# One step of a recurrent cell on one core: tanh straight from the gates, cell update behind it, 250 steps per pass of the loop

## What is computed

```
i = sigmoid(x_t @ U_i + b_i + h @ V_i)
g = tanh   (x_t @ U_c + b_c + h @ V_c)
o = sigmoid(x_t @ U_o + b_o + h @ V_o)
c = h * c + i * g
h = o * tanh(c)
```

## Time and profile before

| | us |
|---|---|
| runs: median (lowest to highest) | 21,944.94 (21,944.29 to 21,952.03) |
| the profiled execution, first to last instruction | 21,945.0 |
| recurrent steps in it, first tanh of the cell (L2048) to the last | 10,610.8 to 21,884.0 |
| TensorE busy over the span | 14,346.5 (65%) |
| VectorE busy | 11,129.5 (51%) |
| ScalarE busy | 7,575.7 (35%) |

### The profile page before, as it was taken

How to read it: one execution, slowest core, us unless ns; L and a number is a source line. 1 busy time by engine, 2 the same in 40 slices (tenths; PEclk the granted TensorE clock), 3 DMA queues, 4 the chain that set the end, 5 groups by cost and what they waited for, 6 DMA issues and landing times. The chain is left out here.

```text
span 21945.0 us, 718236 instructions
## 1 busy us (share of the span) xinstructions
PE 14346.5 (65%) x259448; PEld 11105.6 (51%) x259449; DVE 11129.5 (51%) x57848; ACT 7575.7 (35%) x56505; POOL 6072.3 (28%) x6737
## 2 busy tenths in 40 slices
PE   5417878714864565656777777777777777777776
PEld 3212246512543444444566666666666666666665
DVE  6416666631125545454555555555555555555555
ACT  0007841100110020100455555555555555555554
POOL 1676666675526747476000000000000000000000
PEclk9558977757986777777555555555555555555555
DMA  0000012301013333333000000000000000000000
GB/s 29 15 5 5 1 48 82 74 14 44 24 41 103 102 76 102 75 103 86 6 4 4 4 4 4 4 4 4 4 4 4 4 4 4 4 4 4 4 4 15
DMA packets 344758, 617.89 MB, mean 28 GB/s; under 512 B 152419, under 2 KB 222154, under 8 KB 340328
## 3 DMA queue, kind: packets, MB, share of 16 engines
q0 software_dynamic: 251520, 473.04, 8.5%
q1 hardware_dynamic: 89704, 98.43, 1.4%
HBM read 506.71 MB, written 64.29 MB: 26 GB/s over the span
## 5 line engine op out<-in xcount | busy, mean ns | idle before, releaser
L2024 PE MATMUL lr_Z<-ls_h,ls_V 128*128 128x1 f16 x225000 | 7186.5, 166 | 3316.4 <-DVE ls_h L2071 2623.7
L2024 PEld LDWEIGHTS lr_Z<-ls_h,ls_V 128*128 128x128 f16 x225000 | 6667.9, 105 | 4152.9 <-DVE ls_h L2071 3442.9
L2065 DVE SCALAR_TENSOR_TENSOR ls_c<-ls_S,ls_hc 128x1 f32<-128x1 f32 x12500 | 2374.0, 220 | 4116.6 <-ACT ls_S L2041 4116.6
L2040 ACT ACTIVATE ls_S<-lr_Z 128x1 f32<-128x1 f32 x12500 | 2070.6, 171 | 5260.5 <-PE lr_Z L2024 5260.5
L1985 POOL COPY ls_HT<-ls_h 128x50 f32 x250 | 56.3, 225 | 11233.4 <-DVE ls_h L2073 11233.4
L620 PE MATMUL prop_sum<-prop_G,prop_S 128*128 128x256 f32 x5040 | 1894.5, 555 | 1676.1 <-DMA prop_G<-hop_table,prop_idx 1276.1
L607 POOL DMA_INDIRECT prop_G<-hop_table,prop_idx x2520 | 2386.5, 947 | 1355.1 <-issue 804.5
L620 PEld LDWEIGHTS prop_sum<-prop_G,prop_S 128*128 128x128 f32 x5040 | 1426.1, 290 | 2144.4 <-issue 991.3
L2071 DVE TENSOR_TENSOR ls_h<-ls_S,ls_th 128x1 f16<-128x1 f32 x12500 | 1879.9, 163 | 817.4 <-ACT ls_th L2048 49.4
L2048 ACT ACTIVATE ls_th<-ls_c 128x1 f32<-128x1 f32 x12500 | 2098.4, 199 | 0.0
L2045 ACT ACTIVATE ls_S<-lr_Z 128x1 f32<-128x1 f32 x12500 | 2068.7, 171 | 0.0
(11 more groups left out here) (407 smaller groups left out, 15623.5 us busy)
## 6 DMA issues: line engine op xcount, KB each, us to landing
prop_G<-hop_table,prop_idx POOLq DMA_INDIRECT x2520
hop_table<-gnn_H SPq DMA_DIRECT2D x3, 6400.0 KB, 20.3
me_W<-in_L_ffn_W SPq DMA_DIRECT2D x16, 1024.0 KB, 10.9
moe_out<-me_Ys SPq DMA_DIRECT2D x108, 128.0 KB, 1.7
gm_AG<-gat_atable,gm_idx POOLq DMA_INDIRECT x840
gs_G<-gat_table,gs_idx POOLq DMA_INDIRECT x840
sd_records<-sc_ring_recsd,sc_ring_placesd POOLq DMA_INDIRECT x784, 2.1
ss_records<-me_ring_recss,me_ring_placess POOLq DMA_INDIRECT x432, 2.1
```

The source lines that it names most:

```text
L2024: mm = nc.tensor.matmul(Z[hf][bank][:, col:col + 1], (V2 if part == "21" else V1)[:, q, ROWS.index(row), :], hx[:, prev, q:q + 1], start=F ...
L2040: nc.scalar.activation(S[:, s % 2, m:m + 1], Z[hf][m][:, col:col + 1], ACT.Sigmoid, scale=back)
L2065: nc.vector.scalar_tensor_tensor(c[:, e, m:m + 1], S[:, e, KD + m:KD + m + 1], S[:, e, m:m + 1], hc[:, m:m + 1], ALU.mult, ALU.add).then_i ...
```

## The change

What it does:
- ScalarE makes tanh(c) itself from the gates, as tanh(g * i + hc): input g, scale i, bias hc, all 128x1 in memory. It waits for hc at the start of a step and for its own gate activations before each tanh.
- Its order becomes g0, i0, g1, i1, tanh 0, o0, tanh 1, o1. VectorE's h1 waits for o0 and o1.
- VectorE still makes c, for hc only. h2 is made per half, as tanh * o - h1 in one operation of the kind of L2065, each with its own semaphore, ahead of h. TensorE waits for each half of h2 apart, and only ahead of the first matmul that needs a new one, so 4 waits stand in a step instead of 36.
- h1 and h2 are kept for two steps instead of 50.
- One pass of the loop has 250 steps in parts of 125, so there are 25 passes instead of 125, and `ahead` is 48 matmuls of 125 columns per part.
- The table of activation functions is loaded once ahead of the loop by an instruction of its own.

```diff
-HALF = 25
+HALF = 125
 BODY = 2 * HALF
...
-        h1 = ph.sb("h1", [P, BODY, KD], F16)
-        h2 = ph.sb("h2", [P, BODY, KD], F16)
+        h1 = ph.sb("h1", [P, 2, KD], F16)
+        h2 = ph.sb("h2", [P, 2, KD], F16)
...
-                            hf, prev = s // HALF, (s - 1) % BODY
+                            hf, prev = s // HALF, (s - 1) % 2
...
-                                hx, made = (h2, h2_made) if part == "12" else (h1, h1_made[q])
-                                if (part == "12", q) not in waited:
-
+                                hx, made = (h2, h2_made[q]) if part == "12" else (h1, h1_made[q])
+                                if made not in waited:
                                     pe.wait_ge(made, i * BODY + s + 1)
                                     waited.append(made)
...
+                    nc.scalar.preload_act_table(ACT.Sigmoid)
                     with act.Fori(0, N // BODY) as i:
                         for s in range(BODY):
-                            hf, col, t = s // HALF, s % HALF * KD, i * BODY + s
+                            hf, col, t, e = s // HALF, s % HALF * KD, i * BODY + s, s % 2
+                            act.wait_ge(hc_made, t + 1)
                             for m in range(KD):
                                 act.wait_ge(z[m], t + 1)
-                                nc.scalar.activation(S[:, s % 2, m:m + 1], Z[hf][m][:, col:col + 1], ACT.Sigmoid, scale=back)
-                                nc.scalar.activation(S[:, s % 2, KD + m:KD + m + 1], Z[hf][m][:, col + 1:col + 2], ACT.Tanh,
-                                                     scale=back).then_inc(gates[m], 1)
+                                nc.scalar.activation(S[:, e, KD + m:KD + m + 1], Z[hf][m][:, col + 1:col + 2], ACT.Tanh, scale=back)
+                                nc.scalar.activation(S[:, e, m:m + 1], Z[hf][m][:, col:col + 1], ACT.Sigmoid, scale=back).then_inc(gates[m], 1)
                             for m in range(KD):
+                                act.wait_ge(gates[m], t + 1)
+                                nc.scalar.activation(th[:, e, m:m + 1], S[:, e, KD + m:KD + m + 1], ACT.Tanh, bias=hc[:, m:m + 1],
+                                                     scale=S[:, e, m:m + 1])
                                 act.wait_ge(z[2 + m], t + 1)
-                                nc.scalar.activation(S[:, s % 2, 2 * KD + m:2 * KD + m + 1], Z[hf][2 + m][:, col:col + 1], ACT.Sigmoid, scale=back)
-                            for m in range(KD):
-                                act.wait_ge(cell[m], t + 1)
-                                nc.scalar.activation(th[:, s % 2, m:m + 1], c[:, s % 2, m:m + 1], ACT.Tanh).then_inc(tanh_made[m], 1)
+                                nc.scalar.activation(S[:, e, 2 * KD + m:2 * KD + m + 1], Z[hf][2 + m][:, col:col + 1], ACT.Sigmoid,
+                                                     scale=back).then_inc(o_made[m], 1)
...
-
-                                nc.vector.scalar_tensor_tensor(c[:, e, m:m + 1], S[:, e, KD + m:KD + m + 1], S[:, e, m:m + 1], hc[:, m:m + 1],
-                                                               ALU.mult, ALU.add).then_inc(cell[m], 1)
+                                cell = nc.vector.scalar_tensor_tensor(c[:, e, m:m + 1], S[:, e, KD + m:KD + m + 1], S[:, e, m:m + 1],
+                                                                      hc[:, m:m + 1], ALU.mult, ALU.add)
+                            cell.then_inc(c_made, 1)
...
                             for m in range(KD):
-                                dve.wait_ge(tanh_made[m], t + 1)
-                                nc.vector.tensor_tensor(h1[:, s, m:m + 1], S[:, e, 2 * KD + m:2 * KD + m + 1], th[:, e, m:m + 1],
+                                dve.wait_ge(o_made[m], t + 1)
+                                nc.vector.tensor_tensor(h1[:, e, m:m + 1], S[:, e, 2 * KD + m:2 * KD + m + 1], th[:, e, m:m + 1],
                                                         ALU.mult).then_inc(h1_made[m], 1)
+                            for m in range(KD):
+                                dve.wait_ge(h1_made[m], t + 2)
+                                nc.vector.scalar_tensor_tensor(h2[:, e, m:m + 1], th[:, e, m:m + 1], S[:, e, 2 * KD + m:2 * KD + m + 1],
+                                                               h1[:, e, m:m + 1], ALU.mult, ALU.subtract).then_inc(h2_made[m], 1)
                             nc.vector.tensor_tensor(h[:, s, :], S[:, e, 2 * KD:M6], th[:, e, :], ALU.mult).then_inc(h_made, 1)
                             dve.wait_ge(h_made, t + 1)
-                            nc.vector.tensor_tensor(h2[:, s, :], h[:, s, :], h1[:, s, :], ALU.subtract).then_inc(h2_made, 1)
+                            dve.wait_ge(c_made, t + 1)
                             nc.vector.tensor_tensor(hc[:], h[:, s, :], c[:, e, :], ALU.mult).then_inc(hc_made, 1)
```

More of the change, by code:

```diff
@@ L1975, in lstm_layer @@
             z = [pr.sem(f"z{g}") for g in range(BANKS)]
-            gates, cell, tanh_made, h1_made = ([pr.sem(f"{n}{j}") for j in range(KD)] for n in ("gates", "cell", "tanh", "h1_"))
-            h_made, h2_made, hc_made, kept = (pr.sem(n) for n in ("h", "h2", "hc", "kept"))
+            gates, o_made, h1_made, h2_made = ([pr.sem(f"{n}{j}") for j in range(KD)] for n in ("gates", "o", "h1_", "h2_"))
+            c_made, h_made, hc_made, kept = (pr.sem(n) for n in ("c", "h", "hc", "kept"))
             with pr.block() as block:
@@ L2053, in _ @@
                     for m in range(KD):
-                        nc.vector.memset(h1[:, BODY - 1, m:m + 1], 0.0).then_inc(h1_made[m], 1)
-                    nc.vector.memset(h2[:, BODY - 1, :], 0.0).then_inc(h2_made, 1)
+                        nc.vector.memset(h1[:, 1, m:m + 1], 0.0).then_inc(h1_made[m], 1)
+                        nc.vector.memset(h2[:, 1, m:m + 1], 0.0).then_inc(h2_made[m], 1)
                     nc.vector.memset(hc[:], 0.0).then_inc(hc_made, 1)
```

## The result

The changed kernel takes 22,775.75 us (22,771.88 to 22,779.15) against 21,944.61 of the kernel before (21,940.15 to 21,952.03): a ratio of 1.0379, 95% interval 1.0364 to 1.0394, slower. The forecast was 22,800 (22,350 to 23,300). The profiled execution has 22,769.8, so 824.8 more than the 21,945.0 of before.

The account below looks back on a forecast made before the run. The bound was a ring of dependent small operations, 1.70 us per step, plus the loop's turns. 21,945 + 1,370 for longer steps - 516 for fewer turns + 5 at the start = 22,800 us, range 22,350 to 23,300.

Parts of the forecast that it names:

- The ring: Recurrent stage: dependent small operations across TensorE, VectorE and ScalarE, 1.70 us once round, 6,250 times, plus the loop's turns.
- Fewer turns, -516: Recurrent loop: turns after the first pass go from 124 to 24, 100 x 5.16 us saved.
- Table load, 0: Loop's turn: the 1.28 us load lies wholly beside TensorE's stall, so taking it out saves 0.
- Tanh 0.38: ScalarE's cell tanh: 0.20 us plus 0.09 for each of two operands in memory; next activation starts 0.29 after it.
- First h1 at 0.77: VectorE's first h1 starts 0.77 us after the step's first gate, where it was 0.78.
- Second half 0.36 behind: VectorE's second h1 starts 0.36 us behind the first, where it was 0.14.
- 18th matmul at 0.90: TensorE's 18th matmul of a step can start 0.90 us after the first h1 starts.
- two waits +0.07: ScalarE ahead of g0: waits for both hc and the gates' matmuls add 0.07 us (bounds 0 and 0.09).
- The sum: Whole step: 0.77 + 1.17 = 1.94 us, taken as 1.92, +0.22 per step, +1,370 over 6,226 steps; total 22,800.
- B: Rival on ScalarE's tanh: both operands cost one read, tanh 0.29, step 1.74, total 21,680 us; chance 0.12.
- C: Rival on ScalarE's tanh: operands cost nothing, tanh stays 0.20, step 1.54, total 20,430 us; chance 0.06.
- D: Rival on VectorE: hc is late and holds the gate, step 2.00 to 2.03, total 23,300 to 23,500 us; chance 0.08.

Follow-up runs that it names:

- loop_alone: Kernel before with 250 steps per pass (parts of 125) and nothing else of the change: 23,122.7 us against 23,641.5, ratio 0.978.
- the run with one operand: Changed kernel with the cell tanh's scale a constant and hc still its bias: 23,289.4 us, where the kernel before takes 23,641.5.
- the run with none: Changed kernel with bias and scale of the cell tanh as constants: 22,200.0 us, where the kernel before takes 23,641.5.
- new_step_short_pass: Changed kernel with 50 steps per pass, as before: 24,969.7 us, +1,328 against the kernel before, ratio 1.056.
- hc_wait_at_tanh: Changed kernel with ScalarE's wait for hc moved from the step's start to the first tanh: 22,400.2 us against 21,963.9 of the kernel before, ratio 1.020.
- low_half_alone: Kernel before with h2 made per half in one operation ahead of h, each half with its own wait: 21,878.9 us against 21,963.9, ratio 0.9963.
- the attempt at a better order: Kernel before with 250 steps per pass, h2 per half and ScalarE's order o0 tanh0 o1 tanh1: 21,299.4 us against 21,963.9, ratio 0.9701.
- table_load_alone: Kernel before with the activation table load taken out of the loop and nothing else: 21,964.8 us against 21,963.9, ratio 1.0001.

## Why the prediction was right, point by point

**What bounds it.** The ring was the right picture: the changes of a step's time in the eight runs above are those of the ring, and no engine became the bound (TensorE is busy 73% of the stage in the changed kernel). TensorE's granted clock is 0.50 in it from 12,000 to 15,000 and from 18,000 to 21,000 us, as before.

**Fewer turns, -516.** Right: -514 in the trace of the changed kernel, -519 by the loop alone. A turn did not get cheaper: it costs between 5.1 and 5.7 in all ten traces, with passes of 50 steps and of 250.

**Table load, 0, and work ahead, 0 in the loop.** Right, the first measured by itself, the second by the steps of 1.700 in loop_alone. The first tanh of the stage comes 3.6 later; 5 were in the sum, for the wider matmuls at the start.

**Tanh 0.38.** Right: 0.386, and the o-gate starts 0.29 after it. This was the step that carried the forecast, and the row that decided it was VectorE's, not ScalarE's. That row gave 0.07 for a second operand; the 0.09 that was taken was the price of ScalarE's first one once more, a guess that the run with one operand confirms. By the Trainium skill, "ScalarE: Activation LUTs", section "What ACT_TABLE_LOAD costs", each pointer operand adds about 93 ns; the runs agree, 91 and 92.

**First h1 at 0.77.** It is at 0.74. The four gate activations start 0.07, 0.05, 0.05 apart, not 0.07 each, but the tanh waits for the semaphore of its gate, to 0.27, so only 0.01 of that arrives; the rest is the o-gate, which lasts 0.15 behind a tanh, not 0.17.

**Second half 0.36 behind, 18th matmul at 0.90, two waits +0.07.** 0.33, 0.89 and +0.07, and the next gate 1.16 behind the first h1 where 1.17 was forecast. The second half of h2 is made 0.14 behind the first, as forecast. The mechanism was the one that shows, with TensorE waiting twice inside a step, for the second h1 and for the second half of h2. Three narrow windows on the matmuls of the step above show it:

```profile
18002.16 0.38 PE L2023 MATMUL lr_Z<-ls_h,ls_V 128*128 128x1 f16 x8 [0.58 <-DVE ls_h L2072]
...
18002.49 0.38 PE L2023 MATMUL lr_Z<-ls_h,ls_V 128*128 128x1 f16 x8
...
18002.78 0.27 PE L2023 MATMUL lr_Z<-ls_h,ls_V 128*128 128x1 f16 x4
```

At the pace of each group of eight the 9th matmul would start at .40 and the 17th at .73; they start at .49 and .78. Against the kernel before, the first h1 gains 0.03, the 18th matmul comes 0.17 later behind it, and the second wait ahead of the first gate costs 0.07: together the 0.20.

**The sum.** The step was put at 1.92 and is 1.90: 0.02 x 6,226 = 125 us too much. Left out were the longer steps, 88 us more than before. The two errors nearly cancel. Luck is in the 1.92 too: the terms as they stand give 1.94, and the 0.02 was taken off for rounding, without a row. With 1.94 the sum is some 22,930, still in the range, but 150 too long; the terms that were too long are those of the first h1 (0.03) and of what follows it (0.01). So the 24 us between 22,800 and 22,776 say less for the sum than its terms do.

**The rivals.** B is excluded by the run with one operand. C is what the run with none shows, 1.533 against its 1.54: had the operands been free, the change would have done what it says. D did not come as the rule: the first gate starts 0.12 after hc has ended in the step shown (18002.82 + 0.16 = .98 to 18003.10). The waits of the changed kernel, 12,000 to 22,500 us, name hc 130 times:

```profile
ACT ls_S L2041 <- PE lr_Z L2023: 4700.1, 5293, 6.6
...
ACT ls_S L2041 <- DVE ls_hc L2081: 115.2, 130, 0.9
```

Over the whole stage these are 150 gates, at six places of a pass. At two of them (50 gates) hc is 0.16 late and the gate 0.08 to 0.09: there D is real, and they are among the longer steps below. At the other four the gate is not late.

**What was missed: the longer steps.** In each pass of 250 the same 18 steps are 0.08 to 0.35 longer, in every pass alike. Two of them, near the 85th and the 97th of a pass:

```profile
11744.66 0.16 DVE L2072 TENSOR_TENSOR ls_h<-ls_S,ls_th 128x1 f16<-128x1 f32 x1 [0.17 <-ACT ls_S L2048]
11745.11 0.35 DVE L2076 SCALAR_TENSOR_TENSOR ls_h<-ls_th,ls_S,ls_h 128x1 f16<-128x1 f32 x2 [0.29 <-issue]
```

```profile
11766.81 0.17 ACT L2042 ACTIVATE ls_S<-lr_Z 128x1 f32<-128x1 f32 x1
11767.09 0.17 ACT L2041 ACTIVATE ls_S<-lr_Z 128x1 f32<-128x1 f32 x1
```

VectorE stands 0.29 ahead of L2076 for nothing that the profile shows, and ScalarE starts its third gate 0.28 behind the second, where it is else 0.05. The runs narrow it. It isn't the length of the pass: loop_alone has none, and new_step_short_pass has them at the same first four places. Of the 18 places, 12 are ScalarE's: three that come again every 64 steps (the distances numbered 19, 32, 45 of a pass, then 83, 96, 109, and so on). Where the second wait at the start of a step is moved (hc_wait_at_tanh), only 4 of the 12 are left, 100 steps instead of 300. The other 6 are VectorE's; 4 of them stay in that run. VectorE's come with the longer list of operations per step: low_half_alone has one per pass of 50, the kernel before none. Fixed places in a pass, and the distance of 64 steps, point to something tied to the place in the written-out instructions, such as how they are supplied. That is argued, not shown: no run changed the supply alone, and the cause stays open.

## What to carry to other kernels

In a ring of operations one column wide, count what each operand in memory costs before folding work into an activation: here the first h1 comes 0.56 behind the first gate without the two reads and 0.74 with them, where the kernel with the cell update had 0.78, and the reads are paid once more by the second half, which is queued behind the first. Look for what an operation is really queued behind; the update that was removed was within 0.03 of being hidden. Halves that run one behind the other must be costed to the last reader of the second half: the changed kernel lost there more than the first half had won, the attempt at a better order as much.

## What the runs showed of the hardware that was not expected

- Activations that stand ready in ScalarE's queue start 0.05 apart, not 0.07, but they end 0.06 to 0.07 apart either way, since the later ones last up to 0.19 instead of 0.17 (the four gates of the step shown). The o-gate behind the longer tanh lasts 0.15 in the changed kernel and 0.17 in hc_wait_at_tanh; why is open.
- Steps at fixed places of a written-out body lose mostly 0.08 to 0.36, on ScalarE or on VectorE, and where the engine stops the profile has no releaser, in all seven kernels that make the low part per half, and in none of the three with VectorE's list of before. The cause is open.
- Two chips run the same recurrent step to the nanosecond (1.700 in loop_alone and in table_load_alone), but the first tanh of the cell is at 12,290 us on one and at 10,612 us on the other. A time stated for one of them doesn't hold on the other; a difference in this stage does.
